# Local attention: row maxima from 32-query blocks for four heads at once, and a band applied by VectorE instead of mask products on TensorE

## The reference, cut to what matters

```python
# 16 sequences, T = 512, 16 heads of 8, WINDOW = 32
scores = einsum('bhqd,bhkd->bhqk', Q, K) / sqrt(8)
allowed = (col <= row) & (row - col < 32)     # a query sees itself and the 31 keys before it
scores = where(allowed, scores, -inf)
attn = softmax(scores, axis=-1)
out = einsum('bhqk,bhkd->bhqd', attn, V)
```

## Time and profile before

| | |
|---|---|
| median of 3 runs | 2966.3 us (2964.46 to 2972.68) |
| span of the profiled execution | 3206.8 us, 240.5 us above that median |
| TensorE busy in the span | 2461.8 us (77%), weight loads 1580.8 us (49%) |
| VectorE busy | 2183.2 us (68%) |
| ScalarE busy | 1621.6 us (51%) |
| GpSimd busy | 1506.0 us (47%) |
| TensorE's granted clock, mean | 0.892 of full speed |

### The profile page before, as it was taken

The page is one execution under the profiler, slowest core; times in us unless marked ns, Lnnn a source line. Parts: engine busy times, 40 slices in busy tenths (PEclk is TensorE's granted clock), DMA queues, the critical chain, the costliest instruction groups (busy, mean ns, idle before and its releaser), DMA issues.

```text
span 3206.8 us, 74414 instructions
## 1 busy us (share of the span) xinstructions
PE 2461.8 (77%) x24646; PEld 1580.8 (49%) x24646; DVE 2183.2 (68%) x6265; ACT 1621.6 (51%) x3370; POOL 1506.0 (47%) x1644
## 2 busy tenths in 40 slices
PE   2378859888989587723779579999999999958881
PEld 1266636666667466612668423333333333327770
DVE  3476757666666355566877578888888888836665
ACT  1245624444445255402457437666667667636660
POOL 4752054555443456556420364565566561135551
PEclk9989979899889689955889779999999999979995
DMA  7133222222222133232322111111111111012225
GB/s 162 55 93 105 87 83 65 68 68 70 58 63 62 36 104 107 72 93 83 91 86 83 51 57 47 37 45 51 38 45 51 38 41 42 13 44 73 71 73 167
DMA packets 250055, 222.86 MB, mean 69 GB/s; under 512 B 67078, under 2 KB 230668, under 8 KB 249164
## 3 DMA queue, kind: packets, MB, share of 16 engines
q1 hardware_dynamic: 216028, 148.82, 17.0%
q0 software_dynamic: 33664, 69.27, 7.1%
HBM read 114.00 MB, written 107.53 MB: 69 GB/s over the span
## 4 chain that ended last, share of the span: by engine, by line
PE 51%; DVE 14%; issue 12%; ACT 8%; another core or an unknown queue 6%; DMA 3%; SPq 3%; POOL 2%; ACTq 1%; DVEq 0%; POOLq 0%
PE PS L567 8%; PE PS L764 7%; PE PS L571 6%; PE PS L733 5%; PE PS L712 5%; PE PS L660 4%; ACT arena L913 3%; DVE mxs L1654 3%; ACT arena L970 2%; DVE xr L1346 2%; PE PS L716 2%; PE PS L782 2%; PE PS L720 2%; PE PS L741 2%
## 5 line engine op out<-in xcount | busy, mean ns | idle before, releaser
L1031 ACT ACTIVATE arena<-PS 128x512 f32<-128x512 f32 (+1 forms) x1344 | 702.8, 587 | 345.8 <-PE PS L733 175.5
L1174 POOL DMA_INDIRECT slot_inputs<-xs,slots x512 | 509.6, 995 | 545.8 <-PE PS L733 224.7
L1654 DVE TENSOR_REDUCE mxs<-PS 128x1 f16<-128x512 f32 x1024 | 651.4, 686 | 121.9 <-PE PS L712 111.9
L1248 POOL DMA_INDIRECT G<-block_outputs,places x256 | 252.9, 988 | 565.9 <-DMA block_outputs<-arena 292.4
L913 ACT ACTIVATE arena<-PS 128x256 f16<-128x256 f32 (+2 forms) x586 | 255.9, 442 | 375.2 <-remote 144.9
L712 PE MATMUL PS<-w,q 96*128 96x512 f16 x1024 | 402.2, 395 | 38.0 <-DVE mxs L1654 36.4
L1183 POOL DMA_INDIRECT choice_outputs<-arena x284 | 301.2, 1061 | 238.5 <-DVE arena L1567 88.1
L733 PE MATMUL PS<-q,w 100*128 100x512 f16 x1024 | 394.7, 388 | 18.4 <-ACT arena L1031 15.4
L1658 DVE TENSOR_REDUCE mxs<-PS 128x2 f16<-128x320 f32 x512 | 241.8, 492 | 211.4 <-PE PS L720 201.1
L571 PE MATMUL PS<-ident,arena 128*128 128x128 f32 x1084 | 212.8, 300 | 149.9 <-DMA arena<-slot_inputs 62.7
L1567 DVE TENSOR_TENSOR arena<-PS,arena 128x256 f16<-128x256 f32 x284 | 120.0, 422 | 281.2 <-ACT arena L913 258.1
(11 more groups left out here) (216 smaller groups left out, 4387.8 us busy)
## 6 DMA issues: line engine op xcount, KB each, us to landing
arena<-slot_inputs SPq DMA_DIRECT2D x284, 129.0 KB
block_outputs<-arena SPq DMA_DIRECT2D x142, 128.0 KB
qk_parts<-qk SPq DMA_DIRECT2D x64, 256.0 KB
G<-choice_outputs SPq DMA_DIRECT2D x64, 256.0 KB
q<-qk_parts SPq DMA_DIRECT2D x128, 96.0 KB
slot_inputs<-xs,slots POOLq DMA_INDIRECT x512
qk_parts<-qk SPq DMA_DIRECT2D x64, 128.0 KB
W<-qk_parts SPq DMA_DIRECT2D x128, 48.0 KB
```

Of the source, the lines that this page charges most:

```text
L1031: activate(pT[:, u % PTR, 0:n], PS[:, SC0 + u % NSC[a], 0:n], ACT.Exp, scale=SCALE).then_inc(s_pe, 1)
L1174: g.indirect_dma_start(Xs, bass.IndirectOffsetOnAxis(ap=slots[:, s, c, k:k + 1], axis=0), xs[:, n % XSR, c if f % 2 else 0, k], None).then ...
L1654: vec.tensor_reduce(mxs[:, m % 2, p % NT, QROWS + col:QROWS + col + 1], PS[:, MX0 + u % NMX], AX, ALU.max)\
```

## The change

Maxima: the two units for each head become one unit for two blocks of 128 queries and four heads, made at even p only, so eight for each sequence. A unit is one identity product with a mask of 512 columns and eight products in column tiles, each of 32 queries with the 64 keys of four heads (256 columns). VectorE reduces the unit's 512 columns to eight columns of maxima.

Scores: both mask products go. The exponentials are taken of unmasked scores, shifted by the same maxima, and VectorE's new `window` takes, in place, the minimum of the exponentials and a table that holds 1e38 inside the band and 0 outside. `values` waits for `s_pk`, which `window` raises, where it waited for `s_pe`. `window(t, p - 1)` stands at the end of VectorE's position p, behind its maxima, hook and `late`.

```diff
-KB = P + WIN
+KB = 2 * WIN
+BIG = 1e38
-        maskq = sb("maskq", [P, NT, KB], BF16)
-        maskd = sb("maskd", [P, P], BF16)
-        maskp = sb("maskp", [P, WIN], BF16)
+        maskq = sb("maskq", [P, 2, KB], BF16)
+        keepd = sb("keepd", [P, P])
+        keepp = sb("keepp", [P, WIN])
...
                 def maxima(m, p, part):                          # TensorE
+                    if not full and (part or p % 2):
+                        return
...
-                    o = PS[:, MX0 + u % NMX, 0:2 * KB]
-                    mm(o, identb[:], flat(maskq[:, 2 * part:2 * part + 2]), start=True, stop=False)
-                    for i in range(2):
-                        b = 2 * part + i
-                        lo = 0 if b else WIN
-                        ins = mm(o[:, i * KB + lo:(i + 1) * KB], q3[r, m % 2, p // HG, b * P:(b + 1) * P],
-                                 strip(a, m, p)[r, b * P - WIN + lo:(b + 1) * P], start=False, stop=i == 1)
+                    g, half = p // HG, p % HG // 2
+                    o = PS[:, MX0 + u % NMX].rearrange("p (b j k) -> p b j k", b=2, j=HG)
...
+                    mm(PS[:, MX0 + u % NMX], identb[:], mask, start=True, stop=False)
+                    for b in range(2):
+                        for i in range(P // WIN):
+                            at = (2 * half + b) * P + i * WIN
+                            lo = 0 if at else WIN
+                            ins = mm(o[ST * i:ST * (i + 1), b, :, lo:KB], q3[r, m % 2, g, at:at + WIN],
+                                     (kzf if a else kzw)[r, (m * NG + g) % KR, :, at - WIN + lo:at + WIN], start=False,
+                                     stop=b == 1, tile_position=(0, ST * i))
...
                 def scores(s, p, part):                          # TensorE
-                        mm(o, identb[:], maskd[:].unsqueeze(1).broadcast_to([P, NT, P]), start=True, stop=False)
...
-                        mm(o, identb[:], maskp[:].unsqueeze(1).broadcast_to([P, NT - 1, WIN]), start=True, stop=False)
...
                 def values(s, p):                                # TensorE
-                    pe.wait_ge(s_pe, u + HG + 1)
+                    pe.wait_ge(s_pk, u + HG + 1)
...
+                def window(s, p):                                # VectorE
+                    u, n = exps(a, s, p), NT - 1
+                    v.wait_ge(s_pe, u + 1)
+                    probs = pT[:, u % PTR].rearrange("p (b q) -> p b q", b=NT)
+                    vec.tensor_tensor(probs, probs, bcast(keepd[:], NT, 1), ALU.min).then_inc(s_pk, 1)
+                    if p % HG == HG - 1:
+                        v.wait_ge(s_pe, u + 2)
+                        probs = pT[:, (u + 1) % PTR, 0:n * WIN].rearrange("p (b q) -> p b q", b=n)
+                        vec.tensor_tensor(probs, probs, bcast(keepp[:], n, 1), ALU.min).then_inc(s_pk, 1)
...
                         late(t if p else t - 1, (p - 1) % POS)
+                        if not full and valid(t if p else t - 1):
+                            window(t if p else t - 1, (p - 1) % POS)
```

More of the change, by code:

```diff
@@ L288, in build @@
         s_pe = sem("probs_ready")
+        s_pk = sem("probs_in_window")
         s_pv = sem("values_in_psum")
@@ L318, in maxes @@
         def maxes(a, m, p):
-            return (m * POS + p) * 2 if a == 0 else SEQS * POS * 2 + (m * POS + p) * HG
+            return (m * POS + p) // 2 if a == 0 else SEQS * POS // 2 + (m * POS + p) * HG
         def exps(a, s, p):
@@ L714, in maxima @@
                         return
-                    o = PS[:, MX0 + u % NMX, 0:2 * KB]
-                    mm(o, identb[:], flat(maskq[:, 2 * part:2 * part + 2]), start=True, stop=False)
-                    for i in range(2):
-                        b = 2 * part + i
-                        lo = 0 if b else WIN
-                        ins = mm(o[:, i * KB + lo:(i + 1) * KB], q3[r, m % 2, p // HG, b * P:(b + 1) * P],
-                                 strip(a, m, p)[r, b * P - WIN + lo:(b + 1) * P], start=False, stop=i == 1)
+                    g, half = p // HG, p % HG // 2
+                    o = PS[:, MX0 + u % NMX].rearrange("p (b j k) -> p b j k", b=2, j=HG)
+                    if half:
+                        mask = maskq[:, 1].unsqueeze(1).broadcast_to([P, 2 * HG, KB])
+                    else:
+                        mask = maskq[:].unsqueeze(2).broadcast_to([P, 2, HG, KB])
+                    mm(PS[:, MX0 + u % NMX], identb[:], mask, start=True, stop=False)
[6 more added lines that the diff above has]
+                                     stop=b == 1, tile_position=(0, ST * i))
                     ins.then_inc(s_ms, 1)
@@ L737, in scores @@
                     if part == 0:
-                        mm(o, identb[:], maskd[:].unsqueeze(1).broadcast_to([P, NT, P]), start=True, stop=False)
                         for b in range(NT):
                             c = slice(b * P, (b + 1) * P)
-                            ins = mm(o[:, c], strip(a, s, p)[r, c], q3[r, s % 2, g, c], start=False, stop=b == NT - 1)
+                            ins = mm(o[:, c], strip(a, s, p)[r, c], q3[r, s % 2, g, c], start=b == 0, stop=b == NT - 1)
                     else:
                         o = o[:, 0:(NT - 1) * WIN]
-                        mm(o, identb[:], maskp[:].unsqueeze(1).broadcast_to([P, NT - 1, WIN]), start=True, stop=False)
                         for b in range(1, NT):
@@ L748, in scores @@
                                          strip(a, s, g * HG + j)[r, b * P - WIN:b * P],
-                                         q3[r, s % 2, g, b * P:b * P + WIN], start=False, stop=b == NT - 1,
+                                         q3[r, s % 2, g, b * P:b * P + WIN], start=b == 1, stop=b == NT - 1,
                                          tile_position=(0, ST * j))
@@ L1155, in masks @@
                 step(g.memset(maskq[:], 0.0))
[L1156 to L1162, removed]
+                for i in range(P // WIN):
+                    keep(maskq[ST * i:ST * (i + 1)], ALU.is_ge, NEG, -1, [[0, 2], [1, KB]], -1)
+                    keep(maskq[ST * i:ST * (i + 1)], ALU.is_ge, NEG, WIN, [[0, 2], [-1, KB]], 1)
+                step(g.memset(maskq[0:WIN, 0, 0:WIN], NEG))
+                step(g.memset(keepd[:], BIG))
+                keep(keepd[:], ALU.is_ge, 0.0, 0, [[1, P]], -1)
+                keep(keepd[:], ALU.is_ge, 0.0, WIN - 1, [[-1, P]], 1)
+                step(g.memset(keepp[:], BIG))
                 for j in range(HG):
-                    keep(maskp[ST * j:ST * (j + 1)], ALU.is_ge, NEG, -1, [[-1, WIN]], 1)
+                    keep(keepp[ST * j:ST * (j + 1)], ALU.is_ge, 0.0, -1, [[-1, WIN]], 1)
                 pool.sem_inc(s_con, 1)
@@ L1648, in maxima @@
                 def maxima(m, p, part):
+                    if not full and p % 2:
+                        return
                     u = maxes(a, m, p) + part
@@ L1656, in maxima @@
                     else:
+                        g, half = p // HG, p % HG // 2
                         with nc.allow_low_precision(reason="shift of a softmax, in f16 where it enters the scores"):
-                            vec.tensor_reduce(mxs[:, m % 2, 2 * part:2 * part + 2, QROWS + p], PS[:, MX0 + u % NMX, 0:2 * KB]
-                                              .rearrange("p (b k) -> p b k", k=KB), AX, ALU.max).then_inc(s_mx, 1)
+                            vec.tensor_reduce(mxs[:, m % 2, 2 * half:2 * half + 2, QROWS + g * HG:QROWS + (g + 1) * HG],
+                                              PS[:, MX0 + u % NMX].rearrange("p (b j k) -> p b j k", b=2, j=HG), AX, ALU.max)\
+                               .then_inc(s_mx, 1)
+                def window(s, p):
[7 more added lines that the diff above has]
+                        vec.tensor_tensor(probs, probs, bcast(keepp[:], n, 1), ALU.min).then_inc(s_pk, 1)
                 def normed(s, gq):
@@ L1759, in attention @@
                         if valid(ahead(t, p)[0]):
-                            for part in range(HG // 2 if full else 1, HG if full else 2):
+                            for part in range(HG // 2 if full else 1, HG if full else 1):
                                 maxima(*ahead(t, p), part)
                         late(t if p else t - 1, (p - 1) % POS)
+                        if not full and valid(t if p else t - 1):
+                            window(t if p else t - 1, (p - 1) % POS)
             routers(0)
```

## The result

The changed kernel takes 3075.7 us (median of 4 runs, 3071.79 to 3085.03) against 2966.55: a ratio of 1.0364 [1.0346, 1.0382], 109 us slower. The forecast was 3010, 44 us slower. The sign and the range were right; the rise is two and a half times the one forecast.

A forecast was written before the change was run, and what follows sets the result against it. TensorE was taken to pace the kernel, VectorE following with room. VectorE's work, stalls and half clock made 41.8 us a sequence against 39.1: +43 us over 16, span 3250, less the carried 240.5, rounded to 3010; range 2915 to 3085.

The forecast's parts named there:

- the base: Local attention of the kernel before, read from its first profile: 625.2 us for 16 sequences, 39.1 us each.
- the pauses in L788: TensorE's "issue" waits, 2.7 us a sequence, perhaps from profiling; without them in timed runs, up to 43 us more, 3053.
- TensorE's terms: Per sequence at full clock: 12.0 us of maxima and masks removed, eight units of 0.64 us added, 6.9 us shorter.
- VectorE's terms: Per sequence: old maxima (15.1 us) go, reductions (5.1) and minima (11.1 and 1.0) come, 29.5 us of work.
- 4.3 + 2.2 + 5.8: Per sequence, us: VectorE's handover stalls, second reductions and waits on its own results, and TensorE's half clock.
- The handover: Once a group `values` waits for its last head's `window`, then VectorE for the next maxima unit: 4.3 us a sequence.
- The clock: TensorE's pauses ahead of `values` lower its granted clock: half clock for 0.45 of the time, 5.8 us a sequence.
- (a): Rival: the clock holds and the handover alone decides, 36.0 us a sequence, -49 us, 2917; chance 0.20.
- (b): Rival: TensorE still paces alone, VectorE ahead each time, 31.5 us a sequence, -122 us, 2844; chance 0.07.
- (c): Rival: the maxima units' strips don't run side by side, 5.3 us a sequence, +85 us on the forecast, 3095; chance 0.07.
- (e): Rival: it cancels, a half-clock share near 0.24 leaving the time within 9 us; chance 0.12.
- (d): Rival: POOL and VectorE block each other at the minima, +10 to +74 us on top, 3050 in the middle; chance 0.07.

The follow-up runs named there:

- the second execution: The kernel before, unedited, profiled a second time: 2975.1 us (one run), span 2973.4 us.
- the maxima alone: Changed kernel with both mask products kept and no minima: 2925.1 us, 0.9824 of the kernel before.
- the last head alone: Changed kernel with minima only for each group's last head and the 32 keys ahead, masks for the other heads: 3005.7 us, 1.012 of the kernel before.
- the minimum first in the position: Changed kernel with `window` moved ahead of the position's maxima, hook and `late`: 2989.1 us, 1.0046 of the kernel before.
- the masks kept: Changed kernel with the mask products put back into the scores beside the minima: 3032.2 us, 1.0223 of the kernel before.
- three heads at the start: Changed kernel with minima only for each group's first three heads, first in the position, masks for the rest: 2962.4 us, 0.9976 of the kernel before.

## Why the prediction was wrong in size and right in mechanism

**The step that failed is the base**: "It takes 625.2 us for 16 sequences, 39.1 us each", together with "I carry the difference over unchanged". The timed kernel has 528.5 us there. Of the 240.5 us between the first span and the median, 96.7 lay inside the very stretch that was being compared, and could not be carried over as if they lay beside it. The prediction did see a part: it named the pauses in L788 and gave 3053 for the case that timed runs lack them. But it priced them alone, at 2.7 us a sequence, and not the clock of 0.89 in the same rows, which made TensorE's own work 5.0 us a sequence longer. And it passed over the waits for something unnamed, ScalarE's above all, which the chain on the first profile's page puts at 6% of the span.

**That the sign came out right is partly luck.** The prediction set a steady sequence after (41.8) against a mean before (39.1, ramps included). Against its own steady sequence before, 42.6 us, the same sum gives (41.8 - 42.6) x 16 = -13 us, a faster kernel. Against the steady sequence of the second execution it gives (41.8 - 34.3) x 16 = +120 us, where 109 were measured.

**A smaller error went the other way.** 41.8 us was worked out for a steady sequence and charged to all sixteen, 668.8 us. The local attention after took 630.3: a steady sequence is 42.3, but the first two and the last are shorter (21.5, 31.7 and 31.1 us, by their maxima). The account: +43.6 forecast in the local attention, +96.7 for the base, -38.5 for the shorter sequences at both ends, makes the +101.8 measured. The remaining 7 us to +109 lie between the spans and the medians: the second execution of the kernel before took 2975.1 us, 8.6 above the median beside the changed kernel.

**TensorE's terms held.** A unit is 0.64 us as forecast. Maxima were to save 8.3 - 5.1 = 3.2 us a sequence; alone they save 3.7. A mask still takes 0.22 from start to start in the trace of the maxima alone (median of 256).

**VectorE's terms held.** 29.5 us a sequence forecast, 266.1 / 9 = 29.6 measured. It stands still for (380.9 - 266.1) / 9 = 12.8 us, where 4.3 + 2.2 + 5.8 = 12.3 were forecast; how that splits into the three no run shows. The minima, forecast at 0.69 and 0.25 us from the earlier trace rows, in the changed kernel (ns, least, median, most):

```profile
L1679 DVE TENSOR_TENSOR arena<-arena,keepd x256: 671/681/803, 427.0 to 1067.3; 128x512 f32<-128x512 f32 x128
L1683 DVE TENSOR_TENSOR arena<-arena,keepp x64: 241/250/314, 432.8 to 1067.9; 128x96 f32<-128x96 f32 x64
```

**The handover held**, as a wait in each of 36 groups, at 1.85 us instead of "two to three". That it and not VectorE's load is the main cause was only argued then; the last head alone and the minimum first in the position show it.

**The clock held**: half clock for 0.45 of the time means 0.775, measured 0.75 in steady sequences and 0.78 over the stretch. How near it came is partly luck: 0.45 was a choice between 0.2 and 0.6, both read from the first execution, and the second has a clock of 1.00 where the 0.2 was read. Nor are the waits at the values shown to be what brings the clock down, since with the masks kept waits nearly as long go with 0.96. The forecast priced the clock at 5.8 us a sequence; the masks kept put it at 4.2 or more, with the reservation made there.

**The rivals.** (a) is out, the clock fell. (b) is out, TensorE waits for VectorE in each group. (c) is out, eight strip products end within the unit's 0.64. (e) is out, the clock stood at half for half of the time. (d) is half true, and at the place where the prediction did not look: VectorE's minima hardly stretch (median 681 ns, at most 803; with three heads at the start at most 973), but POOL's norms do, from a mean of 797 to 890 ns in the changed kernel and 1040 in the one with three heads at the start. In the changed kernel's trace the norms that no minimum overlaps (21 of 60) take 782 to 808 ns, and those that one overlaps up to 1542. L1346's row told of VectorE's side only. So the rule in the Trainium skill ("SBUF — State Buffer", section "Who interferes with whom"), that a VectorE instruction with two SBUF inputs contends with a GpSimd instruction that reads SBUF, agrees with these traces, with POOL as the one that mostly pays. In the changed kernel's steady sequences no wait of TensorE is put down to POOL, so it cost nothing there that the views show; in the one with three heads at the start it costs 15.1 us in nine sequences.

## What to carry to other kernels

Before a base is read from a profile, hold its span against the timed median: where they differ by 8%, see how much of it lies in the stretch to be changed, look for waits that the profile can't name, price that stretch at full clock too, and give the case without it its due chance. Compare steady with steady and whole with whole. Work moved from a full engine to one with room is not free if the full engine must wait for it at the point where its own queue goes on; ask for each such wait whether the other engine is a whole step ahead. And where a tuned engine runs at 95% at full clock, taking work off it buys only what the engines that feed it can follow: half of this change was worth 1.8%, and the other half at best nothing in the seven arrangements of this case that have both.

## What was not expected of the hardware

- Putting the mask products back into the changed kernel made it 43 us faster, the granted clock going from 0.75 to 0.96.
- One program gave two profiles 233 us apart (spans 3206.8 and 2973.4 us), with clocks of 0.89 and 1.00 in nine steady sequences, more pauses ahead of L788 (24.2 against 7.6 us) and, in the first alone, waits of ScalarE for something unnamed. What sets this off is not known; the second agrees with every timed run.
- POOL's small powers stretched with the minima beside them as its norms did: 1675 to 2144 ns and 1039 to 1363 ns in mean, without one more element to work on.
